# A first chunk issued by a written table, and packed 4-bit words loaded three bytes early

## The chip, the cores and the metric

One core of a Trainium2 chip runs the whole block. The metric is the device time of one execution in microseconds; three runs of the kernel before gave 986.47, 990.78 and 992.03, median 990.78. Five engines work side by side: TensorE (PE), VectorE (DVE), ScalarE (ACT), GpSimd (POOL) and SyncE (SP), each with its own queue in order, and they wait for one another by semaphores.

## The reference

`x` has 2048 tokens of 256 numbers. The reference computes

```
x = x + 0.5 * ffn(layernorm(x))
x = x + attention(layernorm(x))        # 16 heads of 16, causal
x = x + 0.5 * ffn(layernorm(x))        # the same weights again
ffn(y) = (gelu(y @ Wg.T) * (y @ Wu.T)) @ Wd.T      # 256 -> 2048 -> 256
W[n, 2c], W[n, 2c+1] = LUT[w[n, c] & 15], LUT[w[n, c] >> 4 & 15], each times a scale per 32
```

`w` is an int32 array with one byte of payload in each word (values 0 to 31), so the three upper bytes of a word are zero. LUT holds the sixteen values 0 to 6 and 0 to -6 of a 4-bit float.

## The kernel before

**Tiling.** Tokens go in four chunks of 512 (`CT`). A feed-forward pass over one chunk makes, for each of 16 tiles of 128 hidden units, a product `gate` and a product `up` (six matmuls of 512 columns each: high and low half of weights and of x), then gelu on ACT, the product on DVE (`product`), its high half on ACT (`high`), its low half on POOL; after 16 tiles come four `down` products of 32 matmuls. Chunk 0 of the first pass is special, for the weights don't exist yet: they are unpacked while it runs. Everything after it (`MAIN`, line 190, and `the_order`) goes by an order that a planner writes out; the change leaves that as it is.

**Weights of chunk 0.** There are 12 pieces (gate, up, gate, up, ... then four of down). A piece is loaded as int32 words, `decode` (DVE, L829 and L835) shifts each nibble to the top of the word and masks it so that the word read as two halves holds a 16-bit float: four operations of 128x512 a piece. `decoded` (POOL, L582) multiplies it with its scales: two operations. `transpose_weights` (PE, L1080) turns two groups of four 128x128 blocks of a piece, `weights_high` (ACT, L696) writes their high half, `weights_low` (DVE, L806) the low one. After 24 such groups come four of the projection matrices. Codes have two buffers, values four, the transposed groups two PSUM banks (`W_BANKS`) that `weights_low` sets free.

**Order in chunk 0.** DVE decodes pieces 0 to 5 ahead of the first tile; `first_chunk` on each engine goes tile by tile: gate n, up n, and behind some tiles two groups of weights and one decode (`behind`, `DECODE_AHEAD`). Before the first tile stands a chain: widest scale over all partitions (`amax_rows`, `amax_on_diagonal`, `amax_everywhere`), mean and variance of x (L796, L800), one over the deviation on POOL (`normalise`), `yn` on DVE (L868), its transposes (L1089), `x_high` on ACT and `x_low` on DVE (L892), which lets gate 0 go.

**Queues of loads.** SP issues gate scales, the four gate pieces, the down words and the two projection matrices. ACT issues the other scales, up piece 0, x of chunk 0, up pieces 1 to 3, waits for the last of them and then issues x of chunks 1 to 3.

Of the kernel before, what the change touches and what calls it, by code (L numbers as in the profile page):

```python
# [5 lines left out]
def macaron_block(nc, x, w_project, w_out, gate_packed, gate_scales, up_packed, up_scales,  # L6
# [10 lines left out]
    f32, f16, i32 = mybir.dt.float32, mybir.dt.float16, mybir.dt.int32  # L17
# [3 lines left out]
    P = 128  # L21
# [5 lines left out]
    CT = 512  # L27
# [20 lines left out]
    with ctx:  # L48
# [83 lines left out]
        s_x = [sem(f"x_in{k}") for k in range(NCH)]  # L132
        s_const = sem("constants")
# [34 lines left out]
        W_BANKS = 2  # L168
        FIRST_PIECES = 2

        behind = [[] for _ in range(NT)]
        for p, n in zip(range(FIRST_PIECES, 3 * NPIECE), (1, 2, 4, 5, 7, 8, 10, 11, 12, 13)):
            behind[n] += [2 * p, 2 * p + 1]
        behind[14] += [6 * NPIECE, 6 * NPIECE + 1]
        behind[15] += [6 * NPIECE + 2, 6 * NPIECE + 3]

        AMAX_TILE = 2
        DECODE_AHEAD = 4

# [274 lines left out]
        def load_packed(queue, m, q):  # L454

            dst, src = ((gate_nat, gate_packed), (up_nat, up_packed))[m]
            queue.dma_start(dst[:, 512 * q:512 * q + 512],
                            src.rearrange("(q p r) c -> q p (r c)", p=P, r=TPC)[q]).then_inc(s_packed[m][q], 16)

        def load_scales(queue, dst, src):  # L460
            queue.dma_start(dst[:, :, :].rearrange("p (q r) b -> p q (r b)", r=TPC),
                            src.rearrange("(q p r) b -> p q (r b)", p=P, r=TPC)).then_inc(s_scales, 16)

# [3 lines left out]
        def _(sp):  # L467
            load_scales(sp, sg, gate_scales)
            for q in range(NPIECE):
                load_packed(sp, 0, q)  # L470
            sp.dma_start(down_nat.rearrange("p (k c) -> p k c", k=KT),
                         down_packed.rearrange("(k p) c -> p k c", p=P)).then_inc(s_down_in, 16)
# [3 lines left out]
                         w_out.rearrange("(m p) d -> p m d", p=P)).then_inc(s_out_in, 16)  # L476

# [73 lines left out]
        def _(pool):  # L551
# [7 lines left out]

            own(pool.memset(ones_row, 1.0))  # L560
# [26 lines left out]
            for n in range(6):  # L587
                decoded(n)
                if n == 0:
                    normalise(pool, own, 0, 0)  # L590
            for n in range(NT):
                pool.wait_ge(s_ihigh, n + 1)
                pool.tensor_tensor(inter[:, 1, n, :], prod_ring[:, n % 3, :], inter[:, 0, n, :],
                                   ALU.subtract).then_inc(s_inter, 1)
                if behind[n] and behind[n][0] // 2 + DECODE_AHEAD < 3 * NPIECE:
                    decoded(behind[n][0] // 2 + DECODE_AHEAD)
                if n == 12:
                    normalise(pool, own, 1, 1)

# [43 lines left out]
        def w_bank(k):  # L643
            return bank(k) if k in (2, 3) else bank(4 + k % W_BANKS)

# [19 lines left out]
        XT_BANKS = ps[:, 6 * 512:8 * 512].rearrange("p (k t) -> p k t", k=KT)  # L665
# [13 lines left out]
        def _(act):  # L679
            load_scales(act, su, up_scales)  # L680
            act.dma_start(sd[:, :, :], down_scales.rearrange("(k p) b -> p k b", p=P)).then_inc(s_scales, 16)
            load_packed(act, 1, 0)
            for k in range(NCH):
                if k == 1:
                    for q in range(1, NPIECE):
                        load_packed(act, 1, q)
                    act.wait_ge(s_packed[1][NPIECE - 1], 16)
                act.dma_start(xres[:, TPC * D * k:TPC * D * (k + 1)].rearrange("p (n d) -> p n d", d=D),
                              x[0, CT * k:CT * (k + 1), :].rearrange("(n p) d -> p n d", p=P)).then_inc(s_x[k], 16)
# [8 lines left out]
            def x_high(job, buf=0):  # L698
                act.wait_ge(s_xt, job + 1)
                act.activation(xT[buf][:, 0, :, :], XT_BANKS, ACT.Copy).then_inc(s_xh, 1)  # L700

            def first_chunk():
                for n in range(NT):
                    act.wait_ge(s_gate, n + 1)
                    act.wait_ge(s_prod, 1 if n < 3 else n - 1)
                    act.activation(gelu_ring[:, n % 3, :], bank(n % 2), ACT.Gelu_apprx_tanh,
                                   scale=gelu_in[:, 0:1]).then_inc(s_gelu, 1)
                    if n:
                        high(0, n - 1)
                    for k in behind[n]:  # L710
                        weights_high(k)
                high(0, NT - 1)
                x_high(1)
# [11 lines left out]
            weights_high(0)  # L725
            weights_high(1)
            x_high(0)
            weights_high(2)
            weights_high(3)
# [46 lines left out]
        def _(dve):  # L776
# [32 lines left out]
            def decode(n):  # L809

                m, q = pieces[n]
                if m < 2:
                    dve.wait_ge(s_packed[m][q], 16)
                elif q == 0:
                    dve.wait_ge(s_down_in, 16)
# [42 lines left out]
            for n in range(TPC):  # L858
                statistics(0, n)
# [3 lines left out]
            decode(1)  # L863
# [3 lines left out]
            for n in range(TPC):  # L867
                last = dve.tensor_scalar(yn[:, n, :], xres[:, D * n:D * n + D], neg_mean[:, n:n + 1], rstd[:, n:n + 1],  # L868
                                         ALU.add, ALU.mult)
            last.then_inc(s_yn, 1)  # L870
            dve.tensor_scalar(kappa[:, :], pow_i[:, 0:1], 2.0 ** (I_POW - X_POW - W_POW), None, ALU.mult)
            dve.tensor_scalar(gelu_in[:, :], pow_r[:, 0:1], 2.0 ** (-X_POW - W_POW), None, ALU.mult)
            own(dve.tensor_scalar(tmp1[:, :], pow_r[:, 0:1], pow_r[:, 1:2], 0.5 * 2.0 ** (-I_POW - W_POW),
# [15 lines left out]

            def x_low(job, buf=0):  # L890
                dve.wait_ge(s_xh, job + 1)
                dve.tensor_tensor(xT[buf][:, 1, :, :], XT_BANKS, xT[buf][:, 0, :, :], ALU.subtract).then_inc(s_xl, 1)  # L892

# [21 lines left out]
            def first_chunk():  # L915
                for n in range(NT):
                    product(0, n)
                    if n == 4:
                        dve.wait_ge(s_yn, 1)
                    if 4 <= n < 4 + TPC:  # L920
                        statistics(1, n - 4)
                        step[0] += 1
                    if n == 4 + TPC:
                        dve.wait_ge(s_dve, step[0])
                        aggregate()
                    if behind[n] and behind[n][0] // 2 + DECODE_AHEAD < 3 * NPIECE:
                        decode(behind[n][0] // 2 + DECODE_AHEAD)
                    if n == AMAX_TILE:
                        projections_amax()
                    if n == AMAX_TILE + 2:  # L930
                        amax_on_diagonal(2, 2)
                    if n == AMAX_TILE + 5:
                        projections_powers()
                    for k in behind[n]:
                        weights_low(k)
                x_low(1)
                for n in range(TPC):
                    residual(0, n)

            decode(2)  # L940
            weights_low(0)
            weights_low(1)
            x_low(0)
            weights_low(2)
            decode(3)
            weights_low(3)
            decode(4)
            decode(5)
            for k in range(1, NCH):
                dve.wait_ge(s_x[k], 16)  # L950
            first_chunk()
# [98 lines left out]
        def _(pe):  # L1050
# [3 lines left out]
            def transpose_weights(k):  # L1054
# [9 lines left out]
                if k >= 4:  # L1064
                    pe.wait_ge(s_wl, k - W_BANKS + 1)
                for a in range(2):
# [16 lines left out]
            def transpose_x(job):  # L1083

                pe.wait_ge(s_yn, job + 1)
                for n in range(TPC):
                    v = yn[:, n, :].rearrange("p (j k) -> p j k", k=KT)
                    for kt in range(KT):
                        last = pe.transpose(XT_BANKS[:, kt, P * n:P * n + P], v[:, :, kt], ident[:, :])  # L1089
                last.then_inc(s_xt, 1)  # L1090
# [39 lines left out]
            def first_chunk():  # L1130
                pe.wait_ge(s_xl, 1)
                for n in range(NT):
# [187 lines left out]
```

## Time and profile before

| what | us |
|---|---|
| median of the three runs | 990.78 |
| the profiled execution's own time | 992.37 |
| its span | 990.6 |
| PE busy | 926.6 (94%) |
| DVE busy | 611.1 (62%) |
| ACT busy | 479.2 (48%) |
| POOL busy | 230.5 (23%) |

The page divides the span into 40 slices of 24.8 us. PE is busy for two tenths of the first slice, eight tenths of the second and nine or more tenths of nearly all the others; the DMA engines are busy for seven tenths of the first slice, at 262 GB/s, and idle in most of the rest. A merged row of a timeline has its start, the time from there to the end of its last instruction, engine, line, operation, what it wrote from what it read, and how many instructions it joins; in brackets stands how long the engine was idle before it and who released it.

### The profile page before, as it was taken

To read this page: it belongs to the slowest core of one execution; us is meant where nothing else is said; L and a number is where in the kernel's file an instruction comes from. 1 tells how busy PE (TensorE), PEld (TensorE's weight loads), DVE (VectorE), ACT (ScalarE), POOL (GpSimd) and SP (SyncE) were. 2 spreads that over 40 slices of the span, in tenths; PEclk is the share of its full clock that TensorE was granted. 3 is DMA by queue.
4 is the path that set the end of the run, shared out by engine and by line. 5 is a ranking of instruction groups with operands and counts; after the bars stand their busy time and mean duration, and the time that the engine had idled before them with its cause. 6 is when DMAs were issued, how large, how long until landed. Compare 5 with 4: busy or idle time off the path is not lost.

```text
span 990.6 us, 16766 instructions
## 1 busy us (share of the span) xinstructions
PE 926.6 (94%) x6726; PEld 408.9 (41%) x6726; DVE 611.1 (62%) x994; ACT 479.2 (48%) x650; POOL 230.5 (23%) x261
## 2 busy tenths in 40 slices
PE   2899999999989999888999989999999998999998
PEld 2456544554534545223544322244442222445444
DVE  6984345756777687677778767768785550242221
ACT  2454242033165330787332389963319999742240
POOL 3663573035002430000432000005200000052240
PEclk9999999999999999899999999999999999999999
DMA  7000050014000060000060000000000000000000
GB/s 262 1 1 1 1 96 11 2 57 52 2 2 2 25 83 2 1 1 2 1 107 2 22 2 2 1 1 1 2 22 2 1 2 2 2 1 1 22 1 21
DMA packets 19755, 20.26 MB, mean 20 GB/s; under 512 B 3040, under 2 KB 18400, under 8 KB 19680
## 3 DMA queue, kind: packets, MB, share of 16 engines
q1 hardware_dynamic: 16192, 15.93, 8.3%
q10 hardware_dynamic: 3488, 3.28, 1.0%
q8 instruction: 54, 0.88, 0.4%
q14 instruction: 21, 0.17, 0.1%
HBM read 12.78 MB, written 6.29 MB: 19 GB/s over the span
## 4 chain that ended last, share of the span: by engine, by line
PE 78%; ACT 6%; DVE 6%; issue 6%; DMA 2%; POOL 1%; SPq 0%; ACTq 0%; DVEq 0%; POOLq 0%
PE ps L1124 12%; PE ps L1095 12%; PE ps L1096 11%; PE ps L1097 11%; PE ps L1274 9%; PE ps L1229 7%; ACT inter L742 6%; PE ps L1125 6%; PE ps L1257 4%; DVE sg L1035 2%; DVE sg L1032 1%; PE ps L1241 1%; PE ps L1200 1%; PE ps L1080 1%; DMA xres<-in_L_attn_x 1%
## 5 line engine op out<-in xcount | busy, mean ns | idle before, releaser
L742 ACT ACTIVATE inter<-ps 128x1024 f32<-128x1024 f32 (+3 forms) x320 | 265.9, 898 | 34.9 <-PE ps L1241 19.3
L637 POOL TENSOR_TENSOR inter<-wreg,inter 128x512 f16<-128x512 f32 x112 | 129.3, 1158 | 644.6 <-ACT inter L723 644.4
L1035 DVE TENSOR_REDUCE sg<-ps 128x2 f32<-128x1024 f32 (+3 forms) x217 | 220.2, 1037 | 49.2 <-PE ps L1241 24.4
L752 ACT ACTIVATE wreg<-ps,gelu_in 128x512 f32<-128x512 f32 x112 | 77.1, 688 | 269.9 <-PE ps L1097 269.8
L1124 PE MATMUL ps<-wd,inter 128*128 128x512 f16 x512 | 170.8, 380 | 0.0
L1032 DVE TENSOR_REDUCE sg<-ps 128x1 f32<-128x512 f32 (+3 forms) x206 | 120.8, 632 | 64.7 <-PE ps L1229 43.7
L901 DVE SCALAR_TENSOR_TENSOR wreg<-ps,kappa,wreg 128x512 f32<-128x512 f32 x128 | 95.6, 748 | 102.8 <-PE ps L1097 97.0
L1274 PE MATMUL ps<-inter,v 128*17 128x512 f32 (+3 forms) x1280 | 150.1, 541 | 0.7
L1125 PE MATMUL ps<-wd,inter 128*128 128x256 f16 x512 | 139.5, 273 | 0.0
L1229 PE MATMUL ps<-kreg,qreg 48*128 48x512 f16 (+3 forms) x640 | 109.6, 355 | 18.4 <-DVE sg L1035 11.6
L1257 PE MATMUL ps<-qreg,kreg 50*128 50x512 f16 (+3 forms) x640 | 110.2, 354 | 16.2 <-ACT inter L742 10.6
L1095 PE MATMUL ps<-xT,wg 128*128 128x512 f16 x256 | 98.4, 384 | 1.9 <-DVE wu L806 1.9
L1096 PE MATMUL ps<-xT,wg 128*128 128x512 f16 x256 | 98.1, 383 | 0.0
L1097 PE MATMUL ps<-xT,wg 128*128 128x512 f16 x256 | 98.1, 383 | 0.0
L1095 PE MATMUL ps<-xT,wu 128*128 128x512 f16 x256 | 97.7, 382 | 0.0
L1096 PE MATMUL ps<-xT,wu 128*128 128x512 f16 x256 | 97.2, 380 | 0.0
L1097 PE MATMUL ps<-xT,wu 128*128 128x512 f16 x256 | 97.0, 379 | 0.0
L723 ACT ACTIVATE inter<-wreg 128x512 f16<-128x512 f32 x128 | 79.5, 621 | 10.4 <-DVE wreg L901 10.4
L1257 PEld LDWEIGHTS ps<-qreg,kreg 50*128 50x128 f16 x640 | 31.6, 93 | 115.9 <-ACT inter L742 103.2
L1229 PEld LDWEIGHTS ps<-kreg,qreg 48*128 48x128 f16 x640 | 29.8, 93 | 117.3 <-DVE sg L1035 42.1
L1124 PEld LDWEIGHTS ps<-wd,inter 128*128 128x128 f16 x512 | 50.0, 98 | 63.7 <-issue 9.7
L742 ACT ACT_TABLE_LOAD x4 | 5.1, 1283 | 103.9 <-PE ps L1125 103.9
(130 smaller groups left out, 890.6 us busy)
## 6 DMA issues: line engine op xcount, KB each, us to landing
qk_split<-oT SPq DMA_DIRECT2D x4, 1024.0 KB, 4.5
kreg<-qk_split SPq DMA_DIRECT2D x24, 128.0 KB, 4.7
qreg<-qk_split SPq DMA_DIRECT2D x24, 128.0 KB, 8.2
xres<-in_L_attn_x ACTq DMA_DIRECT2D x4, 512.0 KB, 5.5
out_x<-xres SPq DMA_DIRECT2D x4, 512.0 KB, 2.9
kreg<-in_L_ffn_gate_W_packed SPq DMA_DIRECT2D x4, 256.0 KB, 5.0
kreg<-in_L_ffn_up_W_packed ACTq DMA_DIRECT2D x4, 256.0 KB, 10.2
kreg<-in_L_ffn_down_W_packed SPq DMA_DIRECT2D x1, 1024.0 KB, 9.6
```

The lines of the kernel that those rows point to most:

```text
L637: pool.tensor_tensor(inter[:, 1, u, :], prod_ring[:, u % 3, :], inter[:, 0, u, :], ALU.subtract).then_inc(s_inter, 1)
L742: act.activation(p_ring[:, pair % 8, :, 0:w], ps[:, 512 * b:512 * b + 1024].rearrange("p (a q) -> p a q", a=2)[:, :, 0:w], ACT.Exp, scale= ...
L1032: dve.tensor_reduce(m_part[:, r, part, col + 8 * a:col + 8 * a + 1], bank(at[a], width), AX.X, ALU.max).then_inc(s_slot_read, 1)
L1035: dve.tensor_reduce(m_part[:, r, part, col:col + 9:8], both[:, :, 0:width], AX.X, ALU.max).then_inc(s_slot_read, 1)
L1095: pe.matmul(dst, w[:, 0, kt, cols], xT[buf][:, 0, kt, :], start=(kt == 0), stop=False)
L1096: pe.matmul(dst, w[:, 0, kt, cols], xT[buf][:, 1, kt, :], start=False, stop=False)
L1097: last = pe.matmul(dst, w[:, 1, kt, cols], xT[buf][:, 0, kt, :], start=False, stop=(kt == KT - 1))
L1124: pe.matmul(down_bank(m), inter[:, 0, n, tok], wd[:, n, :], start=(n == 0), stop=False)
L1125: last = pe.matmul(down_bank(m)[:, 0:D], inter[:, 1, n, tok], wd[:, n, 0:D], start=False, stop=(n == NT - 1))
L1229: last = pe.matmul(bank(at[a], w), qreg[c % 2][rows, pair, q0:q0 + P], kreg[rows, pair, k0:k0 + w], start=True, stop=part < c)
L1257: last = pe.matmul(dst[a], kreg[rows, pair, P * j:P * j + P], qreg[c % 2][rows, pair, q0:CT], start=True, stop=j < TPC * c)
L1274: last = pe.matmul(bank(4, CT - q0, q0)[32 * h:32 * h + HD + 1, :], v1[:, j, GH * g + h, :], p_ring[:, b % 8, h % 2, 0:CT - q0], start=(j ...
```

## The change

Words are loaded from three bytes ahead, so that the payload byte is the top byte of each word in SBUF (the other three are the zero bytes of the word before). Row 0 of a matrix has nothing ahead of it: piece 0 goes in two transfers, rows 1 to 127 and row 0, and GpSimd clears the first word. A piece is unpacked with three operations instead of four. Chunk 0 of all engines follows one list (`first`), made of three tables: which product is followed by which decode, which group of weights and which other step. x of chunk 0 is loaded in two halves, early on both queues, and x of the other chunks last on SP; each quarter of `yn` is signalled, and x is transposed, copied and subtracted in halves. The weights have three PSUM banks. Decode 1 and the decodes behind it move behind `x_low`. ACT runs one gelu of one column early. The 3x3 product of `amax_on_diagonal` has two tensor inputs instead of a tensor and a scalar.

```diff
+        W_BANKS = 3
+        GROUP_AT = (0, 0, 1, 1, 3, 4, 6, 6, 11, 12, 13, 13, 16, 18, 18, 21, 22, 24, 26, 26, 28, 29, 29, 31, 31, 31)
+        DECODE_AT = (0, 0, 1, 3, 6, 10, 13, 14, 20, 23)
+        OTHER_AT = {10: ("statistics", 0), 12: ("statistics", 1), 14: ("statistics", 2), 16: ("statistics", 3),
+                    18: ("widest", 0), 19: ("normalise", 1), 20: ("widest rows", 2), 22: ("widest everywhere", 2),
+                    24: ("powers", 2)}
+        first = []
+        products = [("gate", 0), ("gate", 1)]
+        for n in range(NT):
+            products += [("up", n)] + ([("gate", n + 2)] if n + 2 < NT else [])
+        for i, product in enumerate(products):
+            first.append(product)
+            first += [("decode", 2 + p) for p, k in enumerate(DECODE_AT) if k == i]
+            first += [("weights", 2 + p) for p, k in enumerate(GROUP_AT) if k == i]
+            if i in OTHER_AT:
+                first.append(OTHER_AT[i])
...
+        def load_low_bytes_on_top(queue, dst, src, q, landed):
+            row = 4 * dst.shape[1]
+            to, flat = dst.bitcast(u8), src.rearrange("n c -> (n c)").bitcast(u8)
+            if q:
+                queue.dma_start(to, flat[P * row * q - 3:P * row * (q + 1) - 3].rearrange("(p b) -> p b", b=row))                     .then_inc(landed, 16)
+                return
+            queue.dma_start(to[1:P, :], flat[row - 3:P * row - 3].rearrange("(p b) -> p b", b=row))                 .then_inc(landed, 16)
+            queue.wait_ge(s_pool, 1)
+            queue.dma_start(to[0:1, 3:row], flat[0:row - 3].rearrange("(p b) -> p b", p=1)).then_inc(landed, 16)
...
             load_scales(sp, sg, gate_scales)
-            for q in range(NPIECE):
+            load_packed(sp, 0, 0)
+            load_x(sp, 0, slice(2, TPC), s_x_back)
+            for q in range(1, NPIECE):
                 load_packed(sp, 0, q)
...
+            load_x(act, 0, slice(0, 2), s_x[0])
+            for q in range(NPIECE):
+                load_packed(act, 1, q)
+            act.wait_ge(s_const, 1)
+            act.activation(gelu_ring[:, 2, 0:1], ident[:, 0:1], ACT.Gelu_apprx_tanh)
...
-                for k in range(2):
-                    dve.tensor_scalar(like(code_pair[n % 2][k]), w, 28 - 4 * k, 3, ALU.logical_shift_left,
-                                      ALU.arith_shift_right).then_inc(s_dve, 1)
-                for k in range(2):
-                    step[0] += 1
-                    dve.wait_ge(s_dve, step[0])
-                    c = code_pair[n % 2][k]
-                    last = dve.tensor_scalar(c, c, -0x72000000, None, ALU.bitwise_and)
+                low, high = code_pair[n % 2]
+                dve.tensor_scalar(like(low), w, 4, 3, ALU.logical_shift_left, ALU.arith_shift_right).then_inc(s_dve, 1)
+                dve.tensor_scalar(like(high), w, 3, -0x72000000, ALU.arith_shift_right, ALU.bitwise_and)
+                step[0] += 1
+                dve.wait_ge(s_dve, step[0])
+                last = dve.tensor_scalar(low, low, -0x72000000, None, ALU.bitwise_and)
                 last.then_inc(s_code, 1)
...
-                dve.tensor_scalar(amax_diag[0:count, 0:count], ident[0:count, 0:count], amax_top[0:count, 0:1], None,
-                                  ALU.mult).then_inc(s_amax_diag, 1)
+                dve.tensor_tensor(amax_diag[0:count, 0:count], ident[0:count, 0:count],
+                                  amax_top[0:count, 0:1].to_broadcast([count, count]), ALU.mult)\
+                   .then_inc(s_amax_diag, 1)
...
             aggregate()
-            decode(1)
             powers(1, slice(0, 3), W_POW + FP4_POW)
...
+            weights_low(0)
+            dve.wait_ge(s_xh_first, 1)
+            x_low_half(0)
+            dve.wait_ge(s_xh, 1)
+            x_low_half(1)
+            decode(1)
+            weights_low(1)
...
-            decode(2)
-            weights_low(0)
-            weights_low(1)
-            x_low(0)
-            weights_low(2)
-            decode(3)
-            weights_low(3)
-            decode(4)
-            decode(5)
-            for k in range(1, NCH):
+            first_chunk()
+            for k in range(2, NCH):
                 dve.wait_ge(s_x[k], 16)
-            first_chunk()
...
             transpose_weights(0)
             transpose_weights(1)
-            transpose_x(0)
-            transpose_weights(2)
-            transpose_weights(3)
+            for n in range(TPC):
+                if n < TPC - 1:
+                    pe.wait_ge(s_yn_first, n + 1)
+                else:
+                    pe.wait_ge(s_yn, 1)
+                last = transpose_x(n)
...
                 pe.wait_ge(s_wl, 6 * NPIECE)
                 for m in range(TPC):
+                    if m == 2:
+                        pe.wait_ge(s_wl, len(groups))
+                        pe.wait_ge(s_yn, 2)
+                        for n in range(TPC):
+                            last = transpose_x(n)
+                        last.then_inc(s_xt, 1)
                     for part in range(4):
                         down(0, m, part)
```

## Rows read from the trace of the kernel before

**Rows 1.** Timeline of PE, up to the end of chunk 0.

```profile
18.96 1.98 PE L1089 MATMUL ps<-ident,wreg 128*128 128x128 f32 x8 [7.61 <-DVE wreg L868]
...
24.13 0.58 PE L1095 MATMUL ps<-xT,wg 128*128 128x512 f16 x1 [1.47 <-DVE wu L806]
...
28.08 0.38 PE L1095 MATMUL ps<-xT,wg 128*128 128x512 f16 x1
...
30.67 1.04 PE L1080 MATMUL ps<-ident,v 128*128 128x128 f32 x8
...
37.84 1.94 PE L1080 MATMUL ps<-ident,v 128*128 128x128 f32 x8 [3.55 <-DVE wg L806]
...
107.91 0.38 PE L1095 MATMUL ps<-xT,wg 128*128 128x512 f16 x1
```

**Rows 2.** Waits of PE from 24.2 to 88: us, times, longest.

```profile
PE ps L1080 <- DVE wg L806: 4.8, 3, 3.5
PE ps L1095 <- DVE wu L806: 1.9, 2, 1.5
```

**Rows 3.** Two stretches: length, busy times, granted clock, DMA share, GB/s.

```profile
24.00:27.00 3.00, 2.87 (x8) 1.02 (x8) 3.00 (x7) 0.80 (x2) 1.60 (x2) 1.00 0.00 0
...
37.80:40.80 3.00, 2.96 (x12) 2.23 (x13) 3.00 (x7) 1.37 (x2) 1.39 (x2) 0.54 0.00 0
```

**Rows 4.** Timeline of DVE ahead of the first tile.

```profile
5.65 0.75 DVE L829 TENSOR_SCALAR oT<-kreg 128x512 int32<-128x512 int32 x2
...
7.30 1.03 DVE L842 TENSOR_SCALAR amax_diag<-ident,amax_top 3x3 f32<-3x3 f32 x1
11.79 1.40 DVE L796 BATCH_NORM_STATS2 stats<-xres 128x6 f32<-128x256 f32 x4 [3.45 <-DMA xres<-in_L_attn_x]
...
15.90 3.01 DVE L868 TENSOR_SCALAR wreg<-xres,neg_mean,rstd 128x256 f32<-128x256 f32 x4 [0.30 <-POOLq L538]
...
19.19 0.21 DVE L875 TENSOR_SCALAR s_down<-tmp,pow_r 128x1 f32<-128x1 f32 x1
...
22.10 1.22 DVE L892 TENSOR_TENSOR xT<-ps,xT 128x1024 f16<-128x1024 f32 x1
```

**Rows 5.** Timeline of POOL in the same stretch.

```profile
7.26 2.07 POOL L582 TENSOR_TENSOR v<-oT,sg 128x512 f32<-128x512 f16 x2 [4.72 <-DVE oT L835]
13.70 0.59 POOL L534 TENSOR_SCALAR neg_mean<-mv 128x4 f32<-128x4 f32 x1 [4.37 <-DVE mv L800]
...
15.99 2.12 POOL L582 TENSOR_TENSOR v<-oT,su 128x512 f32<-128x512 f16 x2 [0.18 <-POOL rstd L536]
```

**Rows 6.** Timeline of ACT in the same stretch.

```profile
16.74 1.28 ACT L696 ACT_TABLE_LOAD   x1 [16.74 <-issue]
...
20.98 1.02 ACT L700 ACTIVATE xT<-ps 128x1024 f16<-128x1024 f32 x1 [1.68 <-PE ps L1089]
```

**Rows 7.** First up piece on ACT's queue: issue and landing.

```profile
L457 ACTq DMA_DIRECT2D kreg<-in_L_ffn_up_W_packed x1: 488/488/488, 1.9 to 1.9; - x1
...
DMA to landing us min/median/max: 4.6/4.6/4.6
```

**Rows 8.** x of chunk 0 on ACT's queue: issue and landing.

```profile
L688 ACTq DMA_DIRECT2D xres<-in_L_attn_x x1: 456/456/456, 2.4 to 2.4; - x1
...
DMA to landing us min/median/max: 9.3/9.3/9.3
```

**Rows 9.** DMA issues of the page: KB each, median us to landing.

```profile
kreg<-in_L_ffn_gate_W_packed SPq DMA_DIRECT2D x4, 256.0 KB, 5.0
```

**Rows 10.** DVE from 24 to 68 by line and shape: busy us, mean ns.

```profile
L829 DVE TENSOR_SCALAR oT<-kreg 128x512 int32<-128x512 int32 x18 | 12.9, 754 | 0.0
L835 DVE TENSOR_SCALAR oT<-oT 128x512 int32<-128x512 int32 x18 | 8.6, 517 | 0.0
...
L806 DVE SCALAR_TENSOR_TENSOR wg<-ps,mul_w,wg 128x512 f16<-128x512 f32 x6 | 4.2, 736 | 0.0
L879 DVE TENSOR_REDUCE amax<-kreg 128x1 f32<-128x1536 f32 x1 | 1.7, 1740 | 0.0
L796 DVE BATCH_NORM_STATS2 stats<-xres 128x6 f32<-128x256 f32 x4 | 1.6, 412 | 0.0
```

More of the change, by code:

```diff
@@ L462, in load_scales, with load_x @@
                             src.rearrange("(q p r) b -> p q (r b)", p=P, r=TPC)).then_inc(s_scales, 16)
+        def load_x(queue, c, tiles, landed):
+            queue.dma_start(xres[:, TPC * D * c + D * tiles.start:TPC * D * c + D * tiles.stop]
+                            .rearrange("p (n d) -> p n d", d=D),
+                            x[0, CT * c + P * tiles.start:CT * c + P * tiles.stop, :]
+                            .rearrange("(n p) d -> p n d", p=P)).then_inc(landed, 16)
         ones_row = half_sum[0:3, 0, 0:P]
@@ L476, in _ @@
                          w_out.rearrange("(m p) d -> p m d", p=P)).then_inc(s_out_in, 16)
+            for k in range(1, NCH):
+                load_x(sp, k, slice(0, TPC), s_x[k])
             def stack_source(c, m0, half, part):
@@ L585, in decoded @@
                 last.then_inc(s_vals, 1)
[L587 to L598, printed above, removed]
+            decoded(0)
+            normalise(pool, own, 0, 0)
+            decoded(1)
+            for kind, n in first:
+                if kind == "decode":
+                    decoded(n)
+                elif kind == "up":
+                    pool.wait_ge(s_ihigh, n + 1)
+                    pool.tensor_tensor(inter[:, 1, n, :], prod_ring[:, n % 3, :], inter[:, 0, n, :],
+                                       ALU.subtract).then_inc(s_inter, 1)
+                elif kind == "normalise":
+                    normalise(pool, own, n, JOBS[n][0])
             pool.wait_ge(s_wt, len(groups))
@@ L643, in w_bank @@
         def w_bank(k):
[L644 removed]
+            return bank(4 + k % W_BANKS)
         def group_banks(k):
@@ L663, in down_bank @@
             return bank(n)
-        XT_BANKS = ps[:, 6 * 512:8 * 512].rearrange("p (k t) -> p k t", k=KT)
+        HALF = CT // 2
+        XT_BANKS = [bank(6 + h).rearrange("p (k t) -> p k t", k=KT) for h in range(2)]
         def copy_o(act, n, t):
@@ L696, in weights_high, with x_high_half @@
                 act.activation(high, src, ACT.Copy, scale=factor(k)).then_inc(s_wh, 1)
-            def x_high(job, buf=0):
-                act.wait_ge(s_xt, job + 1)
-                act.activation(xT[buf][:, 0, :, :], XT_BANKS, ACT.Copy).then_inc(s_xh, 1)
+            def x_high_half(half):
+                act.activation(xT[0][:, 0, :, HALF * half:HALF * half + HALF], XT_BANKS[half], ACT.Copy)\
+                   .then_inc(s_xh if half else s_xh_first, 1)
             def first_chunk():
[L703 to L711, printed above, removed]
+                for kind, n in first:
+                    if kind == "gate":
+                        act.wait_ge(s_gate, n + 1)
+                        act.wait_ge(s_prod, 1 if n < 3 else n - 1)
+                        act.activation(gelu_ring[:, n % 3, :], bank(n % 2), ACT.Gelu_apprx_tanh,
+                                       scale=gelu_in[:, 0:1]).then_inc(s_gelu, 1)
+                        if n >= 2:
+                            high(0, n - 2)
+                    elif kind == "weights":
+                        weights_high(n)
+                high(0, NT - 2)
                 high(0, NT - 1)
-                x_high(1)
+                act.wait_ge(s_xt, 2)
+                x_high_half(0)
+                x_high_half(1)
             def high(cc, n, projected=0):
@@ L915, in first_chunk @@
             def first_chunk():
[L916 to L921, printed above, removed]
-                        step[0] += 1
[L923 to L928, printed above, removed]
+                for kind, n in first:
+                    if kind == "up":
+                        product(0, n)
+                    elif kind == "decode":
+                        decode(n)
+                    elif kind == "weights":
+                        weights_low(n)
+                    elif kind == "statistics":
+                        if n == 0:
+                            dve.wait_ge(s_yn, 1)
+                            dve.wait_ge(s_x[1], 16)
+                        statistics(1, n)
+                        step[0] += 1
+                        if n == TPC - 1:
+                            dve.wait_ge(s_dve, step[0])
+                            aggregate()
+                    elif kind == "widest":
@@ L929, in first_chunk @@
                         projections_amax()
-                    if n == AMAX_TILE + 2:
-                        amax_on_diagonal(2, 2)
-                    if n == AMAX_TILE + 5:
+                    elif kind == "widest rows":
+                        amax_on_diagonal(n, 2)
+                    elif kind == "powers":
                         projections_powers()
[L934 to L937, printed above, removed]
+                for n in range(2):
@@ L938, in first_chunk @@
                     residual(0, n)
[L940 to L949 removed]
+                dve.wait_ge(s_xh, 2)
+                x_low_half(0)
+                x_low_half(1)
+                for n in range(2, TPC):
+                    residual(0, n)
+            first_chunk()
@@ L1081, in transpose_weights, with transpose_x @@
                 last.then_inc(s_wt, 1)
[L1083 to L1090, printed above, removed]
+            def transpose_x(n):
+                v = yn[:, n, :].rearrange("p (j k) -> p j k", k=KT)
+                for kt in range(KT):
+                    last = pe.transpose(XT_BANKS[n // 2][:, kt, P * (n % 2):P * (n % 2) + P], v[:, :, kt], ident[:, :])
+                return last
             def three_passes(dst, w, cols, buf=0):
@@ L1131, in first_chunk @@
                 pe.wait_ge(s_xl, 1)
-                for n in range(NT):
-                    pe.wait_ge(s_wl, groups.index(("up", n // 2)) + 1 + (n == 1))
-                    gate(0, n)
-                    up(0, n)
-                    for k in behind[n]:
-                        transpose_weights(k)
-                    if n == AMAX_TILE + 1:
-                        amax_rows(2, slice(3, 5))
-                    if n == AMAX_TILE + 4:
-                        amax_everywhere(2, 2)
-                transpose_x(1)
+                for kind, n in first:
+                    if kind == "gate":
+                        pe.wait_ge(s_wl, groups.index(("gate", n // 2)) + 1)
+                        gate(0, n)
+                    elif kind == "up":
+                        pe.wait_ge(s_wl, groups.index(("up", n // 2)) + 1)
+                        up(0, n)
+                    elif kind == "weights":
+                        transpose_weights(n)
+                    elif kind == "widest rows":
+                        amax_rows(n, slice(3, 5))
+                    elif kind == "widest everywhere":
+                        amax_everywhere(n, 2)
                 pe.wait_ge(s_wl, 6 * NPIECE)
                 for m in range(TPC):
+                    if m == 2:
[4 more added lines that the diff above has]
+                        last.then_inc(s_xt, 1)
                     for part in range(4):
```

62 lines of the change are left out of this document (28 added, 34 removed).

## The prediction

> **What bounds the kernel now.** I read the 40 slices of the page first: PE is busy nine tenths or more nearly everywhere, but two tenths of the first slice and eight of the second, and the change touches only what lies there. So the question is when PE comes out of chunk 0. The timeline of PE gives three marks [rows 1]: gate 0 starts at 24.13, gate 1 at 28.08 (four groups of weights are turned by then), and the first matmul of the next chunk at 107.91. From 107.91 on both kernels issue the same order, PE leads it, and a shift of that mark passes through to the end.
>
> Ahead of 24.13 PE waits for a chain. DVE has finished the widest scale at 7.30 + 1.03 = 8.33, then stands until 11.79, when x lands [rows 4]; statistics and the aggregate take until 13.6, when POOL is released [rows 5], POOL's three small operations until 15.9, `yn` 3.01, transposes 1.98, the ACT copy 1.02, the subtraction 1.22 [rows 1, 4, 6]. Behind 24.13 PE loses time in three ways: it waits 4.8 us at weight transposes for `weights_low`, 3.5 of them in one piece ahead of 37.84 [rows 2]; of the 1.9 us of the other row 1.47 lie before 24.13, so 0.4 count; and it runs slowly twice. From 24.13 to 28.08 twelve matmuls take 3.95 us and the next twelve, up to 30.67, take 2.59 (0.216 each), although the granted clock of the first stretch is recorded as 1.00 (I put the 1.36 on the first six, at 0.43 each); after the 3.5 us pause eight transposes take 1.94 instead of 1.04 [rows 1] and the granted clock is 0.54, the lower level of 1.2 GHz [rows 3]. That is 1.4 us the first time, and half of the 2.8 us of work in the second stretch, 1.4 again. Between 28.08 and 107.91 the losses are 4.8 + 0.4 + 1.4 = 6.6, and some 0.8 of small gaps.
>
> **The head, step by step.** The scales start DVE as before. Decode 0 runs at 0.335 an operation (two merged ones take 0.75, and start 0.67 apart) [rows 4]: three end at 6.66 instead of 6.99. The maximum follows, and the 3x3 product would start at 6.97. Before, this tiny operation took 1.03, just until POOL's first multiplication, begun 0.04 earlier, was through (half of 2.07) [rows 4, 5]. Its successor's form stands in no row. Bounds: 0.2, two thirds of a decode step though it is nine elements, and 1.03. I take 1.03, the row of the same place, since POOL moves up by the same 0.33: DVE is free at 8.0.
>
> On that operation the Trainium skill speaks against the change: "SBUF — State Buffer", section "SBUF: two separate sides", says that a VectorE operation with two SBUF inputs takes the pair of ports shared with GpSimd just as a two-port mode does, and that whoever starts first keeps the other out. By it the new form is held like the old one and nothing is gained; without it the chain would be 0.8 shorter. No row here shows a small operation with two tensor inputs beside a POOL multiplication, so the trace can't decide.
>
> x must be there at 8.0. Its front half now takes the place in ACT's queue of the first up piece, which was issued at 1.9 and landed 4.6 later, at 6.5 [rows 7]; the back half is third on SP, and the median of the gate pieces was 5.0 [rows 9], so 2.3 + 5.0 = 7.3. Before, x was issued at 2.4 and took 9.3 [rows 8]. So the stand from 8.33 to 11.79 is gone, and what is late next is the chain itself: statistics and aggregate 1.8 give 9.8; POOL 2.3 gives 12.1 (it is free at 9.0); powers lie beside it. `yn` took 3.01 because decode values of piece 1 ran on POOL at 15.99 [rows 5]; now POOL has nothing, for decode 1 comes later, so I take 4 x 0.335 = 1.35 (at most 3.0): 13.45. Then DVE holds 0.1 of scalars, `weights_low` 0.67, and two half subtractions of 0.65 (half of 1.22 plus a start): 15.6. Beside it lie the last two transposes (13.5 to 14.0) and ACT's half copy (to 14.7), so only DVE sets the end. ACT's table load of 1.28 [rows 6] is over long before. **Gate 0 starts at 15.7, 8.4 us earlier.**
>
> **The first tiles.** The lead isn't kept whole, for weights 2 and 3 now stand behind gate 0. Gate 0 at the slow rate: 18.3. Decode 1 starts only at 15.6: DVE 16.6, POOL 16.8 to 18.9 (2.1), so PE waits 0.6 and turns two groups between 18.95 and 20.4 (1.98 slow, 0.94 fast, which is 1.04 less the end of the last one; I take the middle). Gate 1 until 21.7. Decode 2 stands behind `weights_low` 1 (0.67) and two scalars (0.45) [rows 4], then meets POOL: about 19.6; POOL 19.8 to 21.9. Weights 4 at 21.95; weights 5 need `weights_low` 2, behind decode 3, which is held by the same POOL work: 22.9. They end at 23.6. In the kernel before, the same amount of PE work (two products of six matmuls, and six groups) was done at 28.08 plus 0.94 for two more groups, 29.0. **The lead is 5.4 us.** Bounds from the pieces: PE's own work without a wait would end at 21.5, every decode operation held for a whole multiplication (1.04 + 0.335 = 1.37) at about 27.
>
> **The rest of chunk 0.** From there both have the same PE work. The table turns weights well before they are used and has a third bank, so the 6.6 us of losses go, if DVE keeps up. Up to `widest rows` PE has 19 products of 1.295 and 11 groups of 0.47 = 29.8 us. DVE has 18 decode operations; before, 36 in this stretch took 12.9 + 8.6 = 21.5, 0.6 each with POOL's holding in it [rows 10]: 10.8; 13 `weights_low` and 9 products at 0.67 (mean 0.74 less the overlap) 14.8; statistics 1.7; the two maxima 1.7 and about 0.6: 29.6 in all. The engines are level. With four operations a piece it would be 33.2, so the fourth is worth up to 3.6 here. Level engines with ordered queues still wait at single places; the maxima (2.3 in one stretch, with PE's transpose behind them) are the likeliest. Bounds are 0 and 13.5 (18 operations at 1.37 put DVE 13.5 us behind); I take 2.1, nearer to 0 because the row's 0.6 already holds the blocking. Small gaps of 0.8 stay as they were. Afterwards DVE has some 16 us of work beside 20.7 of PE. Transposing chunk 1 between down products hides its copy and subtraction; down products and transposes cost the same as before. Row 0's own transfers, the one-word clear and x of chunks 1 to 3 at SP's end lie under PE work; x 1 is read behind the fifth up product.
>
> **Sum.** 5.4 + (6.6 - 2.1) = 9.9 us. The profiled execution took 992.37 around a span of 990.6 and would come to 982.5; from the median 990.78 it is 980.9. I predict 981.
>
> **Rivals.** A: the middle closes and the small product isn't held: 0.8 + 2.1 more, 978. For it: in 64 us PE had five such waits in all [rows 2]. Against it: level loads. B: DVE becomes the bound. If its decode operations cost 0.85 rather than 0.6 (the first kind's mean was 0.75), 18 of them put it 4.5 further back: 985.4. C: the x loads don't come early, because scales, two pieces and x (1.2 MB by 7.3) ask for more than the 262 GB/s of the page's first slice gives in 5 us; x at 11.79 as before would leave 3.8 of the 8.4: 984.7. That is also the case in which the change doesn't do what it says. D, the other side: transfers that start three bytes off a word, as bytes, run much slower. Everything hangs on piece 0, issued at 1.3 and needed at 5.65. The gain is used up when it lands 9.9 later, at 15.6, which is three times the median landing of 5.0 [rows 9]; at four times it lands at 21.3, the head ends 15.6 later, and the time is 996.5. Nothing in the trace speaks for it, but no transfer there is unaligned either.
>
> The Trainium skill, "DMA: Bandwidth & Descriptors", section "How a descriptor splits into AXI transactions", has a row of 2 KB off its boundary touch one more 256-byte unit, nine for eight. By that case D would be an eighth, an estimated 0.5 us on the first landing, and hidden; no row here shows it.
>
> **How the numbers follow.** Forecast (978.5 to 984) 0.53, A 0.17, B 0.15, C 0.08, D 0.04, unnamed 0.03. Half a per cent, 5 us, is about what can be told from no change. B and C lie near that bound, so a third of them counts as no change: faster 0.88, same 0.08, slower 0.04. The range for 8 in 10 takes in A and most of B: 975.5 to 986.5.
>
> **What would show it.** Gate 0 at 15 to 16.5; weights 5 turned by 23 to 25; first matmul of chunk 1 near 98 (96 to 102); no PE wait over 1.5 us behind the third tile save one at the second maximum; 36 decode operations instead of 48; x landed by 8. The prediction is wrong if a packed piece lands after DVE asks for it, if DVE's decode operations average over 0.9 us, or if PE's work behind chunk 0 stretches.

## The result, and the profile after

The changed kernel took 999.51 us (median of 4 runs, 998.35 to 1002.01) against 991.22 for the kernel before in the same comparison. The ratio is 1.0094, 95% interval 1.0063 to 1.0125: slower by 0.9%, where 981 was forecast. The profiled execution took 998.51, its span is 996.8.

The chunk behind the head went nearly as foreseen, the head did not. Four rows of DVE's timeline show where the head broke (start, us to the end, operation, idle time before it and its releaser):

```profile
7.14 0.29 DVE L820 TENSOR_REDUCE amax<-sg 128x1 f32<-128x128 f32 x1 [7.14 <-DMA sd<-in_L_ffn_down_scales]
...
22.60 0.43 DVE L858 TENSOR_SCALAR oT<-kreg 128x512 int32<-128x512 int32 x1 [14.79 <-DMA kreg<-in_L_ffn_gate_W_packed]
...
23.92 1.03 DVE L869 TENSOR_TENSOR amax_diag<-ident,amax_top 3x3 f32<-3x3 f32 x1
24.87 1.38 DVE L825 BATCH_NORM_STATS2 stats<-xres 128x6 f32<-128x256 f32 x4
```

DVE stands for 14.8 us until the first gate piece lands at 22.60; before, it was used at 5.65 [rows 4]. Even the scales, which DVE reduces first, came 2 us late (7.14 here, 5.06 before). x, which set the head before [rows 8], is no longer asked for by anyone who waits. From 22.60 on the head runs as forecast, and PE's timeline has gate 0 at 32.38 (24.13 before) and the first matmul of chunk 1 at 116.52 (107.91 before) [rows 1]:

```profile
32.38 0.61 PE L1131 MATMUL ps<-xT,wg 128*128 128x512 f16 x1 [1.42 <-DVE xT L905]
...
116.52 0.38 PE L1131 MATMUL ps<-xT,wg 128*128 128x512 f16 x1
```

The issues on SP's and ACT's queues say that the transfers, not the engines, are at fault. L471 is the transfer of rows 1 to 127, L473 that of row 0:

```profile
1.28 0.39 SPq L471 DMA_DIRECT2D kreg<-in_L_ffn_gate_W_packed  x1
1.72 6.24 SPq L473 DMA_DIRECT2D kreg<-in_L_ffn_gate_W_packed  x1
8.01 0.40 SPq L480 DMA_DIRECT2D xres<-in_L_attn_x  x1
...
14.75 22.58 SPq L473 DMA_DIRECT2D kreg<-in_L_ffn_down_W_packed  x1
```

```profile
3.03 13.26 ACTq L473 DMA_DIRECT2D kreg<-in_L_ffn_up_W_packed  x1
...
18.89 1.28 ACT L712 ACT_TABLE_LOAD   x1 [18.89 <-issue]
```

The issue behind each 127-row transfer blocks for 6.2, 13.3 and 22.6 us, and everything queued behind it waits, ACT's computing too. The word clear it formally waits for was over at 0.87. The windows (length; busy PE, PEld, DVE, ACT, POOL; granted clock, DMA share, GB/s) show what the DMA engines did meanwhile:

```profile
4.00:6.00 2.00, 0.00 (x0) 0.00 (x0) 0.00 (x0) 0.00 (x0) 0.00 (x0) 1.00 0.19 61
6.00:8.00 2.00, 0.04 (x1) 0.07 (x1) 0.67 (x3) 0.00 (x0) 0.00 (x0) 1.00 0.07 25
...
10.00:14.00 4.00, 0.00 (x0) 0.00 (x0) 0.00 (x0) 0.00 (x0) 0.00 (x0) 1.00 0.54 162
...
22.00:26.00 4.00, 0.58 (x2) 0.49 (x3) 3.37 (x9) 0.00 (x0) 2.07 (x2) 1.00 0.07 25
26.00:30.00 4.00, 2.99 (x13) 2.59 (x14) 2.68 (x16) 0.69 (x1) 1.49 (x3) 1.00 0.07 25
```

A share of 0.06 to 0.07 is one engine of sixteen, at 25 GB/s. The two first pieces are 254 rows of 2 KB, 0.52 MB; at 25 GB/s that is 20.8 us, and 1.3 + 20.8 is 22.1. That it meets 22.60 so closely is partly luck: the sum leaves out what else that engine moved. From 8 to 22 the other transfers ran too, at 90 to 201 GB/s in all.

The idea that 127 rows are not spread over the engines is theory S of the experiments. Its first rival, theory B, blames the bytes: sources or targets that lie off a word.

### The profile page after: what moved, and what is told of

Same layout as the page of the kernel before. It is cut to its first block, busy times and chain, and to the rows that moved or that the text cites. A ratio compares the mean times of both kernels' runs of the same rounds, so it can differ in the third digit from the quotient of the medians.

```text
span 996.8 us, 16782 instructions
## 1 busy us (share of the span) xinstructions
PE 924.5 (93%) x6726; PEld 409.1 (41%) x6726; DVE 605.1 (61%) x984; ACT 478.2 (48%) x652; POOL 230.3 (23%) x262
## 4 chain that ended last, share of the span: by engine, by line
PE 76%; ACT 6%; issue 5%; DVE 5%; DMA 4%; SPq 2%; POOL 1%; ACTq 0%; DVEq 0%; POOLq 0%
PE ps L1160 12%; PE ps L1131 11%; PE ps L1132 11%; PE ps L1133 11%; PE ps L1324 8%; PE ps L1279 7%; PE ps L1161 6%; ACT inter L771 6%; PE ps L1307 4%; DVE sg L1071 2%; DMA kreg<-in_L_ffn_gate_W_packed 2%; DVE sg L1068 1%; PE ps L1291 1%; DMA xres<-in_L_attn_x 1%; PE ps L1250 1%
## 5 line engine op out<-in xcount | busy, mean ns | idle before, releaser
L1307 PE MATMUL ps<-qreg,kreg 50*128 50x512 f16 (+3 forms) x640 | 109.3, 351 | 16.0 <-ACT inter L771 10.4
```

What stands on the lines that cost most here:

```text
L1307: last = pe.matmul(dst[a], kreg[rows, pair, P * j:P * j + P], qreg[c % 2][rows, pair, q0:CT], start=True, stop=j < TPC * c)
```

## The experiments

Ten kernels ran, one of them twice. Where a profiled time stands beside a median, it is of one execution; behind chunk 0 the profiles of all kernels need 879.2 to 883.5 us for the same work, so spans of two profiles that differ by up to 4 us say nothing by themselves, and the first matmul of chunk 1 is the better mark. It has a spread of its own, some 1.6 us between two of the kernels below that differ only in how the first rows are cut up: chunk 1 starts at 95.80 in one and at 97.42 in the other. Gate 0 starts 0.4 apart there, and the eight transposes behind it take 1.09 us in the one and 1.97 in the other, as in the first experiment.

**One transfer of 128 rows.** The first bytes of all rows are left out instead of the first row:

```diff
-            queue.dma_start(to[1:P, :], flat[row - 3:P * row - 3].rearrange("(p b) -> p b", b=row)).then_inc(landed, 16)
             queue.wait_ge(s_pool, 1)
-            queue.dma_start(to[0:1, 3:row], flat[0:row - 3].rearrange("(p b) -> p b", p=1)).then_inc(landed, 16)
+            queue.dma_start(to[:, 3:row], flat[0:P * row].rearrange("(p b) -> p b", b=row)[:, 0:row - 3])
+                 .then_inc(landed, 16)
...
-            own(pool.memset(kflat[0:1, 0:6144].rearrange("p (m c) -> p m c", m=3)[:, :, 0:1], 0))
+            own(pool.memset(kflat[:, 0:6144].rearrange("p (m c) -> p m c", m=3)[:, :, 0:1], 0))
```

> The changed kernel, with pieces 0 loaded in one transfer of 128 rows of 2045 bytes that starts at byte 3 of each row (the first word of each row is cleared before), instead of 127 rows and 1 row. Theory S (split): a transfer of 127 rows isn't spread over the 16 DMA engines, 254 rows of 2 KB of two queues go one behind the other at some 0.085 us a row, which is the 21 us to 22.6. Then this kernel has its first piece by 5 to 6, gate 0 at 15 to 16.5 instead of 32.4, no wait of issues on the queues, and 979 to 985 us. Theory B (bytes): transfers whose source or target lies off a word are slow by themselves. Then the first piece lands at 15 or later and the time stays over 992.

Measured: 979.65 us, ratio 0.9895 (0.9873 to 0.9918); run again in a later comparison, 979.38, ratio 0.9878 (0.9856 to 0.9900). Its timeline of DVE, of PE, and its windows:

```profile
5.59 0.42 DVE L859 TENSOR_SCALAR oT<-kreg 128x512 int32<-128x512 int32 x1
...
6.90 1.03 DVE L870 TENSOR_TENSOR amax_diag<-ident,amax_top 3x3 f32<-3x3 f32 x1
7.86 1.39 DVE L826 BATCH_NORM_STATS2 stats<-xres 128x6 f32<-128x256 f32 x4
...
11.49 1.38 DVE L898 TENSOR_SCALAR wreg<-xres,neg_mean,rstd 128x256 f32<-128x256 f32 x4 [1.18 <-POOLq L564]
```

```profile
15.36 0.61 PE L1132 MATMUL ps<-xT,wg 128*128 128x512 f16 x1 [1.41 <-DVE xT L906]
...
24.43 0.38 PE L1132 MATMUL ps<-xT,wu 128*128 128x512 f16 x1
...
97.12 0.38 PE L1132 MATMUL ps<-xT,wg 128*128 128x512 f16 x1
```

```profile
4.00:6.00 2.00, 0.18 (x1) 0.08 (x1) 1.00 (x5) 1.45 (x2) 0.00 (x0) 1.00 0.95 306
6.00:8.00 2.00, 0.21 (x2) 0.02 (x1) 1.97 (x6) 0.04 (x1) 1.14 (x2) 1.00 1.00 326
```

All sixteen engines work, nothing waits for a load, and gate 0 comes at 15.36. Bytes, and sources or targets three off a word, cost nothing that the time shows: DVE is never held by them in chunk 0. A small cost isn't excluded: the same table with aligned words (below) has 330 and 366 GB/s in the two windows where this one has 306 and 326. Theory B falls, S stands.

**The kernel before with one piece in 127 aligned rows.** Nothing is off a word here:

```diff
+            if q == 0 and m == 0:
+                queue.dma_start(to[1:P, :], rows[1:P, :]).then_inc(s_packed[m][q], 16)
+                queue.dma_start(to[0:1, :], rows[0:1, :]).then_inc(s_packed[m][q], 16)
+                return
             queue.dma_start(to, rows).then_inc(s_packed[m][q], 16)
```

> The kernel before, in which gate piece 0 alone is loaded in two transfers, rows 1 to 127 and row 0, as whole aligned words. Theory S: 127 rows at 0.087 us make 11 us, the piece lands near 13 instead of before 5.65, decode 0 starts 7 us later, the statistics start near 15.6 instead of 11.8, and the time is 993.5 to 996. Theory B: nothing changes, the piece lands by 5.5 and the time is 990 to 992.

Measured: 1000.43 us, ratio 1.0114 (1.0090 to 1.0137). Theory S again, but I had the size wrong: the piece landed at 19.97, not 13, and the time is 4 us above the range. The issue behind the 127 rows blocked for 6.07 us here too, with every word aligned.

```profile
19.97 0.76 DVE L833 TENSOR_SCALAR oT<-kreg 128x512 int32<-128x512 int32 x2 [11.82 <-DMA kreg<-in_L_ffn_gate_W_packed]
```

11 us would be the engine to itself (254 KB at 25 GB/s are 10.4). The windows of this kernel still show 278 GB/s from 2 to 8 and 268 from 8 to 20: the other transfers went on. If a sixteenth of each passes the same engine, the 127 rows share it. That fits the 18 us from issue to landing; no run tests it by itself.

**Other counts of rows.** The changed kernel, whose rows 1 to 127 go in two transfers:

```diff
+            for r0, r1 in ((1, 113), (113, P)):        # and 1 to 120, 121 to 127 in the next one
+                queue.dma_start(to[r0:r1, :], flat[row * r0 - 3:row * r1 - 3].rearrange("(p b) -> p b", b=row))
+                     .then_inc(landed, 16)
```

> The changed kernel, with rows 1 to 127 of the first pieces in two transfers, 112 rows (seven for each of 16 engines) and 15 rows. Theory S (a count that 16 divides is spread, 127 isn't): the first piece is there by 6.5, gate 0 by 16.5, 980 to 983. Theory W (only transfers of all 128 partitions, or that start at partition 0, are spread): as slow as the changed kernel, gate 0 near 32, 998 to 1001.

> The same with 120 rows, 7 rows and 1 row. It tells how the rows are spread: if over the greatest divisor up to 16 (15 engines for 120), the first piece is there by 6.5 as with 112 rows; if only a multiple of 16 is spread, 240 rows of two queues take some 20 us and the first piece lands near 21; over eight engines, by 8.

Measured: 980.53 us, ratio 0.9893 (0.9878 to 0.9908) with 112 and 15; one run of 979.59 with 120 and 7. Gate 0 at 15.53 and 15.12. So neither a start at partition 0 nor all 128 partitions is needed; and the transfer of row 0 alone was innocent, its issue took 0.22 here. 120 isn't a multiple of 16 and is still spread. 127 has no divisor but 1. The Trainium skill, "DMA: Bandwidth & Descriptors", section "Why a DMA increments its semaphore by 16 and not by 1", says just that: a transfer is split over the largest number up to 16 that divides the slowest dimension of its source and its target, and it names 127 partitions as the case of one engine. The counts tried here (128, 120 and 112 against 127) agree. They don't single out the page's rule: 128, 120 and 112 are all multiples of 8, and the small rests of 15 and 7 rows would go unnoticed on one engine, so "multiples of 8 are spread" would give the same times. No run here tells over how many engines 120 rows went.

**The up piece alone in 127 rows,** with gate and down in one transfer each.

> The table with one transfer of 128 rows for gate and down, but up piece 0 in 127 rows and 1 row. Theory S: 127 rows on one engine, shared with its part of everything else, land near 15 to 20 instead of 8; decode 1 is asked for at 15.2, and the other pieces' parts on that engine are late too, scales by some 2 us as in the changed kernel: gate 0 at 16 to 18, time 982 to 988. If only the piece that comes first mattered: gate 0 at 15.4 and 980.

Measured: 991.29 us, ratio 1.0010 (0.9994 to 1.0025), worse than the 982 to 988 I expected: one such transfer undoes the whole gain. From its ACT and DVE timelines:

```profile
3.02 10.01 ACTq L476 DMA_DIRECT2D kreg<-in_L_ffn_up_W_packed  x1
13.06 1.87 ACTq L469 DMA_DIRECT2D kreg<-in_L_ffn_up_W_packed  x3
14.97 1.28 ACT L719 ACT_TABLE_LOAD   x1 [14.97 <-issue]
```

```profile
25.37 0.43 DVE L865 TENSOR_SCALAR oT<-kreg 128x512 int32<-128x512 int32 x1 [6.35 <-DMA kreg<-in_L_ffn_up_W_packed]
```

I had counted the landing only. ACT issues loads and computes in one queue, so the blocked issue held its first `weights_high` to 16.4, gate 0 came at 19.08 (3.7 late), and then PE waited 7.1 us for piece 1.

**The table alone.** Aligned words, four operations, 128 rows. GpSimd clears nothing.

```diff
-                low, high = code_pair[n % 2]
-                dve.tensor_scalar(like(low), w, 4, 3, ALU.logical_shift_left, ALU.arith_shift_right).then_inc(s_dve, 1)
...
+                for k in range(2):
+                    dve.tensor_scalar(like(code_pair[n % 2][k]), w, 28 - 4 * k, 3, ALU.logical_shift_left,
+                                      ALU.arith_shift_right).then_inc(s_dve, 1)
...
```

> The changed kernel with the load and the unpacking of the kernel before: aligned words, 128 rows a transfer, four operations a piece; GpSimd clears nothing. The table alone. Against 979.65 for the table with three operations and 128-row transfers, theory L (VectorE is level with TensorE in the middle, so the fourth operation costs there): 982 to 985, DVE's decodes make PE wait 3 us or more between 23 and 60. Rival F (the fourth operation is free, since it hides like it did in the old order, where three operations changed the median by 0.9): 979.5 to 981.

Measured: 985.28 us, ratio 0.9933 (0.9920 to 0.9946), apart from 0.9895 and 0.9878. PE's waits from gate 0 on, that ahead of gate 0 included, here and then with three operations (us, times, longest):

```profile
PE ps L1192 <- DVE amax L921: 3.3, 1, 3.3
PE ps L1128 <- DVE xT L902: 1.4, 1, 1.4
PE ps L1115 <- POOL v L603: 1.0, 1, 1.0
```

```profile
PE ps L1196 <- DVE amax L925: 1.4, 1, 1.4
PE ps L1132 <- DVE xT L906: 1.4, 1, 1.4
PE ps L1119 <- POOL v L609: 0.7, 1, 0.7
```

Theory L holds, though 985.28 lies just above its range: the fourth operation shows up where DVE has the maxima to do. Chunk 1 starts at 101.06, 3.9 later than with three operations. The wait at the second maximum gives 1.9 of it. Another 1.65 comes behind the wait, which ends at 57.76: there the granted clock is at the lower of its two levels, 1.2 GHz, and matmuls follow one another at 0.43 us instead of 0.22 until 61.3. After the 1.4 us wait of the kernel with three operations it stays at 1.00.

```profile
58.00:62.00 4.00, 4.00 (x15) 2.02 (x13) 2.03 (x7) 1.75 (x3) 3.94 (x5) 0.57 0.03 6
```

**The old order with three operations,** loaded as in the first experiment.

> The kernel before with the load three bytes early in one transfer of 128 rows (the first word of each row cleared) and three operations a piece, order unchanged. Theory S: x still lands near 11.8 and sets the head; behind it decode 1 and 2 stand ahead of gate 0 in DVE's queue with an operation less each (0.7), and the 3.5 us wait before the third tile shrinks by up to 2.5: 987 to 990 us. Theory B: the first piece lands late, over 995 us.

Measured: 989.64 us (10 runs), ratio 0.9991 (0.9977 to 1.0006). Within what was expected, but it is no gain that can be told. The profile has chunk 1 at 104.61, 3.3 earlier, while the medians differ by only 0.9. The two profiled executions explain most of that: this one (988.61) lies 1.0 below its median, and the one of the kernel before (992.37) 1.9 above the median of this comparison, 990.50.

**The old order with x early.**

```diff
-            load_packed(act, 1, 0)
             for k in range(NCH):
                 if k == 1:
-                    for q in range(1, NPIECE):
+                    for q in range(NPIECE):
```

> The kernel before with one edit: x of chunk 0 is issued ahead of up piece 0 on ACT's queue. It separates the early load of x from the table. If x was what set the head, statistics start at 8.3 to 9 instead of 11.8, gate 0 comes 2.8 to 3.4 earlier than 24.13, and the time is 987 to 988.5; the rest of the head's 8.8 us then belongs to the order of decodes. If something else stood behind x, gate 0 stays within 1 us of 24.1 and the time at 990 to 991.5.

Measured: 989.27 us, ratio 0.9981 (0.9971 to 0.9992), some 2 us less than before and above the range I gave. x was what the head waited for, as 8.45 for the statistics says, but gate 0 came only 2.0 earlier (22.12), for ACT still waits at its own loads until 14.9 and DVE then waits for ACT. In this profile chunk 1 starts at 107.38, only 0.5 earlier; with the spread of that mark, what the old order keeps of the 2.0 lies between the 0.5 and the medians' 2.

```profile
8.45 1.40 DVE L795 BATCH_NORM_STATS2 stats<-xres 128x6 f32<-128x256 f32 x4
...
18.60 1.41 DVE L805 SCALAR_TENSOR_TENSOR wg<-ps,mul_w,wg 128x512 f16<-128x512 f32 x2 [1.07 <-ACT wg L695]
```

**The held 3x3 product.** In the first experiment's kernel GpSimd waits for it:

```diff
+            pool.wait_ge(s_amax_diag, 1)
             decoded(0)
```

> The table with one transfer of 128 rows, and GpSimd's first multiplication waits until the 3x3 product of the widest scales is made. Theory H (the 3x3 product with two tensor inputs is held by GpSimd's multiplication, as its 1.03 us with a start 0.04 after it say): it takes 0.2 us, statistics start at 7.1 instead of 7.9, unless x isn't there yet (it lands near 7), gate 0 0.5 to 0.8 earlier than 15.36, 978.8 to 979.5. Rival: the operation is slow by itself, 1.03 again, gate 0 at 15.4 or later.

Measured: 980.26 us, ratio 0.9878 (0.9862 to 0.9894).

```profile
7.04 0.15 DVE L871 TENSOR_TENSOR amax_diag<-ident,amax_top 3x3 f32<-3x3 f32 x1
```

0.15 us instead of 1.03: the operation was held, theory H. But gate 0 moved only from 15.36 to 15.19, because GpSimd's multiplication ends later too (9.50 instead of 8.93), and the time didn't move. Chunk 1 does start 1.3 earlier in this profile, at 95.86, but the edit is hardly the reason: the transposes behind gate 0 run at full rate, as they do with 120 + 7 + 1 rows, where the product still took 1.02. The rows show the repaired kernel first, then this one; the granted clock is recorded as 1.00 in both, and why one gets fast sooner stays open.

```profile
18.77 1.97 PE L1119 MATMUL ps<-ident,v 128*128 128x128 f32 x8 [0.67 <-POOL v L609]
18.59 1.10 PE L1120 MATMUL ps<-ident,v 128*128 128x128 f32 x8 [0.67 <-POOL v L609]
```

**The second maximum later in the list** (with the edit above):

```diff
-                    18: ("widest", 0), 19: ("normalise", 1), 20: ("widest rows", 2), 22: ("widest everywhere", 2),
-                    24: ("powers", 2)}
+                    18: ("widest", 0), 19: ("normalise", 1), 22: ("widest rows", 2), 24: ("widest everywhere", 2),
+                    25: ("powers", 2)}
```

> The table with one transfer of 128 rows, GpSimd's first multiplication behind the 3x3 product, and PE's transpose of the second maximum two products later in the list (its followers 2 and 1 later). Theory L: PE's wait of 1.4 us at that transpose goes, chunk 1 starts 1 to 1.4 earlier, 978 to 979.5, which may be within what is measured. Rival: DVE is behind by as much anyway, the wait turns up at the next weights or products, no change.

> The first experiment's kernel again, beside the one above on the same chip: 979 to 981. What the run above differs by is told against this one.

Measured on one chip: 977.86 us, ratio 0.9867 (0.9849 to 0.9885), beside 979.38 for the one without either edit. PE's one wait behind 15.5 is now

```profile
PE ps L1120 <- POOL v L609: 1.9, 1, 1.9
```

and chunk 1 starts at 93.9 in its profile, 3.4 before that of the kernel beside it (97.27). Only part of this is the edit's. From up 0 on (22.69 here, 24.57 beside) the chunk takes 71.2 instead of 72.7 us, and that 1.5 is the wait at the maximum, which is gone. Most of the rest is a luckier head: gate 0 starts at 14.41 instead of 15.45 and runs at full rate, and the 1.9 us wait is the price of being early at GpSimd.

```profile
14.41 0.39 PE L1133 MATMUL ps<-xT,wg 128*128 128x512 f16 x1 [1.52 <-DVE xT L907]
```

The medians differ by 1.5 as well, but the intervals overlap, so as a gain in time it is likely, not shown. Both beat both kernels.

## Why the prediction was wrong, point by point

**The step that failed** is the premise under "The head": that the pieces land as in the rows of before, and that "row 0's own transfers ... lie under PE work". Splitting off row 0 leaves 127 rows, and I costed the odd transfer of one row and not the one beside it. The first piece landed at 22.6 instead of near 5. Against the repaired load that is 17.0 us at gate 0 (32.38 and 15.36), and 19.4 at chunk 1 (116.52 and 97.12); the medians differ by 19.9.

**Rival D** had the place and the price: piece 0, break-even at a landing of 15.6, and by its arithmetic a landing at 22.6 gives 981 + 17 = 998, where 999.5 was measured. It had the wrong mechanism (bytes off a word), and I gave it 0.04. Worse, I weighed one rule of the Trainium skill's "DMA: Bandwidth & Descriptors" there and did not look on that page for how rows are shared among engines; the sentence that decides this case stands under another heading. That D got so little rested on the lack of any unaligned row in the trace; the trace had no row of 127 partitions either, and I didn't ask.

**The rest of the head was right.** With the load repaired: statistics at 7.86 (8.0 said), `yn` 1.38 us (1.35 said), gate 0 at 15.36 (15.7 said). The 3x3 product took 1.03 as taken: it takes 1.03 beside GpSimd's multiplication and 0.15 ahead of it. The rule of the Trainium skill, "SBUF — State Buffer", section "SBUF: two separate sides", on VectorE operations with two SBUF inputs is borne out by this. **Rival C** rested on a sum that doesn't come out: 1.2 MB in 5 us are 240 GB/s, less than the 262 named beside it; with the load repaired 306 and 326 GB/s were moved from 4 to 8 and x was there by 7.86.

**The first tiles:** weights 5 turned by 24.4 instead of 23.6. I let PE speed up behind gate 0; in the repaired kernel gate 1 still takes 2.56 us for its six matmuls, and the eight transposes ahead of it 1.97, with a granted clock recorded as 1.00. Where PE did speed up there (120 + 7 + 1 rows), weights 5 were turned by 23.1.

**The rest of chunk 0:** from there 72.7 us to chunk 1 (74.4 said). Engines level, and one wait at the second maximum, 1.4 us (2.1 said). The upper bound there should have read 13.7, not 13.5 (29.6 + 13.9 - 29.8). In the changed kernel itself x of chunk 1, late behind the blocked issues (DVE waits 1.8 us for it until 58.87), and other waits made it 84.1 from gate 0 against 81.8 when repaired. The fourth operation: 3.6 said for the middle and 0.3 for the head, 0.38% to 0.55% measured between the ratio 0.9933 and the two of the repaired kernel, 3.8 to 5.5 us. My 3.9 had no term for the slower clock behind the longer wait (1.65 us), and the wait itself grew by 1.9.

**The sum** was 981; the kernel that does what the prediction took the change to do measured 979.65 and 979.38. So close a hit is helped by two misses that cancel: PE was through with weights 5 by 0.8 us later than said, and the rest of chunk 0 took 1.7 us less.

## What to carry to other kernels

Count the rows of every transfer, not only its bytes: peeling one row off 128 leaves a prime number, and one engine of sixteen carries it. Shorten all rows by the awkward bytes, or cut the rest into counts with a large divisor. When an edit splits a transfer, price both parts and also what stands behind them in the issuing queue, above all where that queue computes as well.

## What the runs showed of the hardware that I had not expected

An issue behind a transfer on one engine blocks for long: 6.2, 13.3 and 22.6 us in the changed kernel, 6.1 with aligned words, so a slow transfer stops issues that have nothing to do with it. One DMA engine moved 25 GB/s, in 2 KB rows (6 to 8 us) as in 4 KB ones (30 to 37). A byte-wise load with sources or targets three bytes off a word costs nothing that any engine waits for: the first gate piece lands 3.5 us after its issue, and 3.4 or 3.5 with aligned words. A VectorE operation on nine elements can take 1.03 us because of a GpSimd multiplication that began 0.04 earlier. PE can run at half rate at the start of its work while the granted clock is recorded as 1.00. And a head start isn't kept by itself: statistics 3.3 us earlier in the old order gave some 2 us in the medians.
